# Weaving the mixtures of one batch with the attention, norm and router of the other in a four-layer gated decoder

## The reference

```
ffn 1 (mixture 1): top 2 of 8 experts by router logits, softmax of the two
    h = gelu(x @ w1[e].T + b1[e])                  # 128 -> 512
    out += weight[e] * (h @ w2[e].T + b2[e])       # 512 -> 128
attention 2: 16 heads of 8, keys masked, softmax(q k / sqrt 8) v @ wo
ffn 2 (mixture 2): best 2 of 4 groups, top 2 of 8 experts, weights normalised
    out += weight[e] * ((silu(x @ gate[e].T) * (x @ up[e].T)) @ w2[e].T)   # 128 -> 256 -> 128
attention 3: 16 heads of 8, no mask, with biases
ffn 3: 64 scalars per token, each through a relu net of 16 units, back to 128
```

## Time and profile before

| | |
|---|---|
| three runs, median (lowest to highest) | 489.1 us (484.35 to 489.6) |
| profiled execution | 487.85 us, span 486.0 us |
| busy share of the span | PE 85%, PEld 65%, DVE 75%, ACT 42%, POOL 40% |
| mean granted TensorE clock | 0.849 |

### The profile page before, as it was taken

One profiled execution on the slowest core, in us unless ns is written; L12 is line 12 of the kernel. 1 busy time (PEld: TensorE's weight loads), 2 busy tenths in 40 slices (PEclk: granted clock), 3 DMA queues, 4 the chain that ended last, 5 costly groups with the idle time before them and its releaser, 6 DMA issues.

```text
span 486.0 us, 5965 instructions
## 1 busy us (share of the span) xinstructions
PE 413.8 (85%) x1988; PEld 317.9 (65%) x1988; DVE 363.8 (75%) x694; ACT 202.2 (42%) x351; POOL 195.7 (40%) x158
## 2 busy tenths in 40 slices
PE   2898988787999999996899996599999957999865
PEld 1586747765666666673599985367666625999834
DVE  5437485686499999978767469699999987674356
ACT  2201313234777666660555422144444313644045
POOL 3101063224688998862010027156666522000052
PEclk9666865857999999997899985799999976998558
DMA  6500000101011111100010000011210000000001
GB/s 199 232 2 0 1 0 1 45 0 43 7 44 43 45 43 32 32 3 0 0 34 1 1 1 0 3 36 34 65 32 1 1 0 2 0 1 1 1 0 45
DMA packets 8640, 12.54 MB, mean 26 GB/s; under 512 B 1132, under 2 KB 4758, under 8 KB 8614
## 3 DMA queue, kind: packets, MB, share of 16 engines
q1 hardware_dynamic: 7984, 11.58, 7.4%
q10 hardware_dynamic: 533, 0.31, 0.2%
q0 software_dynamic: 96, 0.32, 0.2%
HBM read 11.54 MB, written 0.52 MB: 25 GB/s over the span
## 4 chain that ended last, share of the span: by engine, by line
PE 45%; DVE 32%; issue 11%; ACT 7%; POOL 3%; DMA 1%; ACTq 0%; DVEq 0%; POOLq 0%
DVE rhi L1074 8%; PE bank L1569 7%; PE bank L1217 3%; PE bank L1551 3%; PE bank L1218 3%; PE bank L1219 3%; DVE shared L1163 3%; DVE wa L1053 2%; DVE rhi L1166 2%; PE bank L1225 2%; DVE rlo L1080 2%; ACT shared L771 2%; PE bank L1457 2%; PE bank L1460 2%; POOL rstd L364 1%
## 5 line engine op out<-in xcount | busy, mean ns | idle before, releaser
L364 POOL TENSOR_TENSOR rstd<-var,neghalf 128x4 f32<-128x4 f32 x16 | 16.2, 1012 | 173.3 <-DVE var L804 173.3
L427 POOL TENSOR_TENSOR rlo<-shared,rhi 128x512 fp32r<-128x512 f32 x40 | 56.3, 1408 | 45.3 <-DVE rhi L1166 22.7
L1217 PE MATMUL bank<-hhi,wuh 128*128 128x512 f32 x128 | 53.0, 414 | 10.8 <-DVE shared L1163 5.9
L1074 DVE CAST rhi<-shared 128x512 fp32r<-128x512 f32 x48 | 53.4, 1113 | 7.1 <-ACT shared L670 7.0
L670 ACT ACTIVATE shared<-bank,b1s 128x512 f32<-128x512 f32 x64 | 43.9, 687 | 27.5 <-PE bank L1219 25.8
L1218 PE MATMUL bank<-hlo,wuh 128*128 128x512 f32 x128 | 52.3, 409 | 0.0
L1219 PE MATMUL bank<-hhi,wul 128*128 128x512 f32 x128 | 52.1, 407 | 0.0
L1457 PE MATMUL bank<-rhi,wdh 128*128 128x512 f32 x96 | 40.9, 426 | 10.5 <-POOL rlo L427 8.7
L437 POOL TENSOR_TENSOR wb<-wb,wa 128x512 f32<-128x512 f32 x28 | 40.9, 1462 | 14.8 <-DVE wa L1053 14.8
L1133 DVE TENSOR_REDUCE small<-bank 128x6 f32<-128x462 f32 (+1 forms) x48 | 27.8, 579 | 19.4 <-PE bank L1219 19.4
L1080 DVE TENSOR_TENSOR rlo<-shared,rhi 128x512 fp32r<-128x512 f32 x32 | 37.7, 1177 | 5.7 <-ACT rhi L674 5.1
(11 more groups left out here) (276 smaller groups left out, 921.1 us busy)
## 6 DMA issues: line engine op xcount, KB each, us to landing
up_raw<-in_w SPq DMA_DIRECT2D x8, 258.0 KB, 2.7
down_raw<-in_w SPq DMA_DIRECT2D x8, 256.0 KB, 2.8
up_raw<-in_v SPq DMA_DIRECT2D x8, 256.0 KB, 2.6
down_raw<-in_v SPq DMA_DIRECT2D x8, 128.0 KB, 2.7
const<-in_const SPq DMA_DIRECT2D x1, 913.0 KB, 6.9
mats<-in_mats SPq DMA_DIRECT2D x1, 640.0 KB, 5.1
mats<-in_mats SPq DMA_DIRECT2D x1, 576.0 KB, 3.9
x<-in_x SPq DMA_DIRECT2D x2, 256.0 KB, 3.5
```

Source lines behind the costliest of these rows:

```text
L427: nc.gpsimd.tensor_tensor(rlo[n % 4][:, :], ring[n % 4][:, :], rhi[n % 4][:, :].bitcast(F32), ALU.subtract).then_inc(lo, 1)
L1074: V.tensor_copy(rhi[n % 4][:, :], ring[n % 4][:, :]).then_inc(q["hiD"], 1)
L1217: mm(o, lh, rh, start=start, stop=False)
```

## The change

From the first router on, the two batches are one stage apart. Every engine's program is a weave of two step lists made in Python: a main one (a mixture of one batch) and a side one. After main step s, side steps follow until `made >= (s + 1) * n_side / (share * n_main)`. The stages are: mixture 1 of batch 0 beside the first router, the context of attention 3 and its values (15 steps over the first 26 of 65 slots); mixture 1 of batch 1 beside update, norm, attention 2, norm and router 2 of batch 0 (71 steps, 65 slots); mixture 2 of batch 0 beside the same of batch 1 (71 steps, 50 slots); mixture 2 of batch 1 beside attention 3 and the last layer of batch 0 (74 steps, 50 slots); attention 3 and the last layer of batch 1 alone (49 steps).

Other parts:
- Every expert is loaded, rounded and split once for each batch (32 loads instead of 16).
- Gelu and the product with Silu are written back to PSUM. The rounding is by ScalarE from PSUM (in mixture 1 three of four, the fourth by VectorE), all differences are by VectorE from PSUM.
- The weights' rows go to DRAM by a DMA and come back broadcast to 128 partitions (two experts of 512 tokens, 512 KB, in each of 16 DMAs). VectorE weights a group's result straight from PSUM, in mixture 1 with b2 added. The products for b2, the small matmuls of `weights_row` and ScalarE's copies of results (L656) go.
- Attention scores are single fp32 products of 4 heads (32 rows of q and k each, 308 columns), in four groups, instead of three fp32r products in three banks; `kbh`, `kbl`, the splits of q and k go. `kbg` and `vals` get a copy of their own for each attention and batch.
- Mixture 1 has four banks for its hidden products with batch 0 and three with batch 1; mixture 2 has three banks for its halves and one for the result.
- The last layer has one unit of eight on GpSimd, as before seven on ScalarE.

Cut to its core (`...` marks what is left out):

```diff
+HEAD = [[("outN",)], [("update0",)], [("power0",)], [("normal0",)], [("turn0",)], [("hT0",)], [("query",)], [("queryT",)]]
+TILES_BESIDE = [
+    [("score", 0, 0)], [("sub", 0, 0)], [("sub", 0, 1)], [("score", 0, 1)], [("sub", 0, 2)], [("sub", 0, 3)],
+    [("score", 1, 0)], [("sub", 1, 0)], [("sub", 1, 1)], [("score", 1, 1)], [("sub", 1, 2)], [("sub", 1, 3)],
+    [("exp", 0), ("score", 2, 0)],
+    [("exp", 1), ("turn", 0, 0)],
+    [("copy", 0, 0)], [("turn", 0, 1)], [("copy", 0, 1)], [("turn", 0, 2)],
...
+    [("exp", 2)], [("exp", 3), ("turn", 2, 0)],
...
+TAIL = [[("OT",)], [("OTs",)], [("wo",)], [("update1",)], [("power1",)], [("normal1",)], [("turn1",)], [("hT1",)]]
+ROUTE = [[("rest",), ("router",)], [("logits",)], [("router_exp",)], [("groups",)], [("ranks",)], [("weights",)],
+         [("cT",)], [("cTs",)], [("rows",)]]
...
+def weave(main, side, n_main, n_side, share):
+    made = 0
+    for s in range(n_main):
+        next(main)
+        while made < n_side and made < (s + 1) * n_side / (share * n_main):
+            next(side)
+            made += 1
+    for _ in range(made, n_side):
+        next(side)
...
...
+            weave(moe1(0), first_side(), SLOTS1, len(FIRST_SIDE), 0.4)
+            weave(moe1(1), attend(0, 0), SLOTS1, len(steps_of(0, 0)), SHARE)
+            weave(moe2(0), attend(0, 1), SLOTS2, len(steps_of(0, 1)), SHARE)
+            weave(moe2(1), attend(1, 0), SLOTS2, len(steps_of(1, 0)), SHARE)
+            for _ in attend(1, 1):
+                pass
...
+            def load_rows(s, i):
+                sp.wait_ge(written[s], 16)
...
+                sp.dma_start(rowB[:, 2 * i:2 * i + 2, :],
+                             rowd[s, 2 * i:2 * i + 2, :].partition_broadcast(P)).then_inc(rows_in[i], 16)
...
+            def moe1(b):
+                for g in range(N1):
+                    G, eg, c = N1 * b + g, E * b + g // C1, g % C1
+                    if G < LAST[0]:
+                        gelu(G + 1)
+                    yield
+                    high1(G)
+                    if c == 0 and eg > 0:
+                        down_hi(eg + 1)
+                    if c == 2:
+                        up_hi(eg + 2)
+                    yield
+                yield
...
+            def high_and_rest(G):
+                bk = bank[hidden_bank(G)][:, :]
+                if G % 4 == 1:
+                    dve.wait_ge(q["gelu"], G + 1)
+                    V.tensor_copy(rhi[G % 4][:, :], bk).then_inc(q["hiD"], 1)
+                    dve.wait_ge(q["hiD"], high_by_dve(G))
+                else:
+                    dve.wait_ge(q["hiA"], high_by_act(G))
+                V.tensor_tensor(rlo[G % 4][:, :], bk, rhi[G % 4][:, :].bitcast(F32), ALU.subtract).then_inc(q["lo"], 1)
...
+            def moe1(b):
+                for g in range(N1):
+                    G = N1 * b + g
+                    if b == 0 and g + 3 < N1:
+                        hidden1(G + 3)
...
+                    elif b == 1 and g + 2 < N1:
+                        hidden1(G + 2)
+                    yield
+                    down1(G)
+                    yield
+                yield
...
+            def moe2(b):
+                half2(2 * N2 * b)
+                half2(2 * N2 * b + 1)
+                yield
+                for j in range(N2):
+                    J = N2 * b + j
+                    if j + 1 < N2:
+                        half2(2 * J + 2)
+                    yield
+                    if j + 1 < N2:
+                        half2(2 * J + 3)
+                    yield
+                    down2(J)
+                    yield
+                yield
...
-                        mm3(o, tile(qh[b], t), tile(ql[b], t), kbh[b][:, h0:h1, :], kbl[b][:, h0:h1, :],
-                            n == 1, True).then_inc(at["S"], 1)
+                    for g in (2 * half, 2 * half + 1):
+                        score_bank_free(T, g)
+                        rows_g = slice(GR * g, GR * (g + 1))
+                        mm(bank[score_bank(n, b, g)][:, 0:HG * K], tile(qT[b][rows_g, :], t), kbg[n][b][rows_g, :, :],
+                           start=(n == 1), stop=True).then_inc(at["S"], 1)
```

More of the change, by code:

```diff
@@ L192, in flamingo_program @@
         ysb, acc = W1_, W2_
+        qT = W3_
+        gated = [[W3_[b], W4_[b]] for b in range(B)]
         rhi = [sb(f"rhi{i}", [P, S], F32R) for i in range(4)]
@@ new lines, in attend @@
+            def attend(n, b):
+                for step in steps_of(n, b):
+                    for op, *_ in step:
+                        if op == "rows":
+                            for i in range(E // 2):
+                                load_rows(2 + b, i)
+                        elif op == "store":
+                            sp.wait_ge(l3["done"], b + 1)
+                            sp.dma_start(out[b].rearrange("(t p) d -> p t d", p=P), x[b][:, :, :]).then_inc(out_done, 16)
+                    yield
@@ L774, in _, with exponentials @@
[L774 to L783 removed]
+            def exponentials(R, tiles):
+                act.wait_ge(m["sub"], R)
+                nc.scalar.activation(ex[:, tiles, :], lg[:, tiles, :], ACT.Exp).then_inc(m["exp"], 1)
@@ new lines, in first_side @@
+            def first_side():
+                tiles = slice(0, BT)
+                for step in FIRST_SIDE:
+                    for op, *_ in step:
+                        if op == "logits1":
+                            logits(1, tiles, 6)
+                        elif op == "ranks1":
+                            ranks(lg[:, :, :], E, lt8, rank[:, :, :], tiles)
+                            dve.wait_ge(m["exp"], 1)
+                            weights(rank[:, :, :], tiles)
+                    yield
@@ new lines, in first_side @@
+            def first_side():
+                for step in FIRST_SIDE:
+                    for op, *arg in step:
+                        if op == "router1":
+                            pe.wait_ge(m["split"], B)
+                            for b in range(B):
+                                last = router(0, b, 6 + b, 6, NT * b)
+                            last.then_inc(m["lg"], 1)
+                        elif op == "cT1":
+                            pe.wait_ge(m["sub"], 1)
+                            weights_T(1, arg[0], (7, 6)[arg[0]])
+                        elif op == "context":
+                            pe.wait_ge(m["cTs"], B)
+                            context(1)
+                        elif op == "replicate":
+                            replicate(1, arg[0])
+                    yield
```

1442 lines of the change are left out of this document (703 added, 739 removed).

## The result

The change makes the kernel slower: 557.75 us median of 4 runs (548.6 to 558.97) against 489.06 for the kernel before beside it, ratio 1.1325 (95% interval 1.1139 to 1.1511). Forecast were 466 us and a range of 438 to 500. The profiled execution has 556.79 us and a span of 555.0.

A forecast was written before the change was run, and what follows sets the result against it. VectorE was taken to hold both long mixtures, with no engine full in 86.7 us of short stages. Start 103, woven stages 61, 88, 77, 72 and last part 63 sum to 464; with 1.85 more, 466 us, range 438 to 500.

The forecast's parts named there:

- drain: Rival at ScalarE's table switches: each of 19 costs its 1.28 us once more, 490 us in all; chance 0.13.
- ScalarE's sum: ScalarE per chunk of mixture 1: Gelu, roundings and weight work, 1.50 us, with gaps about 1.60.
- Now the stages, each from its fullest engine, plus what the in-order queues lose: Summing step for all stages: fullest engine plus queue losses, the four woven ones at 61, 88, 77 and 72 us.
- The main chain has two chunks of slack: In the woven mixtures: a late side step holds the main step behind it, with two chunks of slack.
- the ring: Mixture 1's loop of down product, hidden product, Gelu, rounding and difference; the main chain was given two chunks of slack.
- First stage: Mixture 1 of batch 0 with router 1, context and values: 56 us of ScalarE plus routing and row wait, 61.
- The row load: First DMA of weight rows in mixture 1, batch 0: about 3 us of wait in VectorE.
- Scores: Attention's sixteen fp32 score products of 308 columns on TensorE: 0.52 us each, by the nearest row.
- The lockstep rival: In the woven mixtures a slot costs main step, side step and hand-over summed: 510 us in all; chance 0.20.
- The clock: TensorE's granted clock from 103 to 400 us: 0.9 or more expected if the forecast is right.
- Tables: ScalarE's function table loads: 19 more than now at 1.28 us each, 24 us.
- VectorE off the mixtures: In both mixtures VectorE loses most roundings and SBUF-only sources; 1.03 us a chunk in mixture 1, 1.71 in mixture 2.

The follow-up runs named there:

- the bare mixture: Changed kernel with all side steps of the three woven stages put behind the mixture instead of between its steps: 645.8 us.
- the swap: Changed kernel with ScalarE's rounding of a mixture 1 chunk put ahead of the next chunk's Gelu: 549.5 us, ratio 1.137 to the kernel before.
- the run with copies: Changed kernel with every exponential from the first router on made a plain copy: 544.8 us, ratio 1.1245 to the kernel before.
- the 468.5 us kernel: Kernel before with both mixtures in PSUM form and the row-spreading product contracting over 128 rows instead of 8: 468.5 us, ratio 0.9661.

## Why the prediction was wrong

- **The costs of single instructions** were right: differences 0.69, Gelu 0.66, rounding 0.60, 24 table loads of 1.28, and where the next activation's input was ready it starts 0.01 to 0.02 us behind the load, so no drain shows. ScalarE's sum was too high: between 150 and 169 us, with the side steps done, four chunks take 5.73 us (1.43 each), of which TensorE's 24 products are 5.5, and ScalarE is busy 16.2 of 19 us, 1.22 a chunk and not 1.50, for its instructions overlap where they stand back to back (one of 0.61 us starts at 159.77, the next at 160.25).
- **"Now the stages, each from its fullest engine, plus what the in-order queues lose"** is the step that failed. It gave 61, 88, 77 and 72; they are 76.7, 128.5, 91.7 and 93.9. Of the 40.5 us missing in the second stage 13 are in the bare mixture (64 for ScalarE's 51), and the side adds 64.5 where 37 had been put down for it and all losses. Two things were missing. The side's chain was never added up as a chain: engine by engine it is 28, 31 and 15 us, in a row it is 80 to 87. And the loss by the queues was guessed at 2 to 5 us for each part, where each side step costs 0.91 us in mixture 1 and 0.68 in mixture 2.
- **"The main chain has two chunks of slack"** holds for batch 0's four banks. With three banks and the Gelu ahead of the rounding the ring closes over two chunks; bare that is 64 / 32 = 2.0 us a chunk instead of 1.43, and in the woven stage the swap takes 11.6 us off. Three banks with the swap were not run bare, so what the banks cost alone is open.
- **First stage.** 32 chunks at 1.43 are 46 us; 61 were forecast, 15 more, and 76.7 came, 31 more. The row load was on the list with 3 us, was measured with 4.13, and nothing comes off when it is taken away; the router costs in the weave what it costs ahead of it, within the stage's spread of 6 us.
- **Scores.** Taken at 0.52; four instructions, two products, are shown in 0.79 us, less the tail 0.63, so 0.32 each. From their start at 197.65 us to that of the product behind them at 198.37 pass 0.72 us, 0.36 for each. The 0.52 was right as a bound and is small beside the rest.
- **The lockstep rival** had the mechanism and the sign. Its price was too low: it added 42 us to the forecast's 298 for the four stages, and 93 came; its 510 us are 48 short. Its chance of 0.20 should have been the largest: the profile of before had no row in which two dependent chains share queues, and the earlier trace rows showed how long the short stages are while no engine is full.
- **The clock.** "TensorE's clock at 0.9 or more from 103 to 400" did not come: 0.86, 0.83 and 0.85. The stages were added up from products at 0.23 us. How much of the miss this is was not measured by itself; extra products that raised it to 0.91 did not make the second stage shorter (129.5 us).
- **Tables.** 12.6 us over three stages by the run with copies, for a term of 24 taken as wholly in ScalarE's load.
- **VectorE off the mixtures** was right and is what the 468.5 us kernel keeps.

What stays open: in the second stage the swap took 11.6 us off and the copies 2.9, and the rest of the 64.5 us that the side adds is not divided. How much of it is waits of a side step, waits of a main step, or the lower clock was not measured by itself.

## What to carry to other kernels

Before weaving two chains into in-order queues, add up each chain's own length with its hand-overs, not its work by engine: the stage is at least the longer one, and here it came near the sum of both (128.5 us for 64 and 87). Make a main ring's slack a number (chunks between one rounding and the same queue's next need of it), and keep an exchange between two engines out of a single step (with such steps the three stages grew by 9, 21 and 11 us). A part of a large change can be right while its order is wrong: try the parts in the old order.

## What the hardware showed unexpectedly

- Between products of 128 rows at a pitch of 0.23 us, one with a contraction of 8 rows takes the time from the start before it to the start behind it from 0.46 to 0.75 us; made 128 high with zeros it is back at 0.46. In mixture 1 that was 108.8 to 102.7 us, in mixture 2 nothing.
- 22 us of extra products in a stage of 128.5 us cost 1.0 us, with the clock going from 0.83 to 0.91; in mixture 2, 11 us of them cost 5.1 and 3.3. And the first stage, with the same instructions, took between 71 and 77 us from run to run, with a clock between 125 and 150 us of 1.00 (run with VectorE's work twice) or 0.79 (the changed kernel).
- The start, with the same code, ended at 98.0 to 99.3 us in the three profiles with a clock of 0.63 between 60 and 100 us, and at 103.2 to 104.6 in those with 0.50.
- GpSimd's weight rests (L389 before, 1514 ns in the earlier trace rows) take 1306 ns in the changed kernel, where VectorE reads PSUM in the mixtures. That comes with the PSUM form and not with the new order: in the kernel before with the PSUM form in mixture 1 alone they take 1361 ns, with it in both mixtures 1303. GpSimd's own differences went with the same change, so VectorE's source is not shown to be the cause by itself.
